# Row norm, turning and first products of eight stages put into one block each, tile by tile

## The reference: a network of four graph layers and four expert layers

```python
def _layernorm(x, axis=-1, eps=1e-05):
    m = jnp.mean(x, axis=axis, keepdims=True)
    v = jnp.var(x, axis=axis, keepdims=True)
    return (x - m) / jnp.sqrt(v + eps)
...
x = x + _L0_gnn_ref(_layernorm(x, axis=-1), edge_index, ...)
x = x + _L0_ffn_ref(_layernorm(x, axis=-1)[None], ...)[0]
x = x + _L1_gnn_ref(_layernorm(x, axis=-1), edge_index, ...)
x = x + _L1_ffn_ref(_layernorm(x, axis=-1)[None], ...)[0]
x = x + _L2_gnn_ref(_layernorm(x, axis=-1), edge_index, ...)
x = x + _L2_ffn_ref(_layernorm(x, axis=-1)[None], ...)[0]
x = x + _L3_gnn_ref(_layernorm(x, axis=-1), edge_index, edge_attr_256, ...)
x = x + _L3_ffn_ref(_layernorm(x, axis=-1)[None], ...)[0]
```

## Time and profile before

| | us |
|---|---|
| time before, median of 3 runs | 6647.78 |
| lowest and highest run | 6633.71, 6653.32 |
| span of the profiled execution | 6654.2 |
| PE busy in it | 4985.8 (75%) |
| DVE busy | 4006.3 (60%) |
| POOL busy | 2796.2 (42%) |
| ACT busy | 2392.6 (36%) |

### The profile page before, as it was taken

How to read it: one execution, slowest core, us unless ns; L and a number is a source line. 1 busy time by engine, 2 the same in 40 slices (tenths; PEclk the granted TensorE clock), 3 DMA queues, 4 the chain that set the end, 5 groups by cost and what they waited for, 6 DMA issues and landing times. The chain is left out here.

```text
span 6654.2 us, 84797 instructions
## 1 busy us (share of the span) xinstructions
PE 4985.8 (75%) x21057; PEld 3321.4 (50%) x21058; DVE 4006.3 (60%) x8393; ACT 2392.6 (36%) x5749; POOL 2796.2 (42%) x2895
## 2 busy tenths in 40 slices
PE   0677669458778667757775788889889994667998
PEld 0444336334436534433343444467678884455776
DVE  5577823457783467766777788821357775892112
ACT  0333312123332234423442555522135552552333
POOL 1577332447740077717771677700047673000000
PEclk9799869779998889988997899989999997897999
DMA  4444233234430144434441222100079995541000
GB/s 92 127 136 135 59 93 119 74 106 136 135 78 15 40 133 136 135 74 133 135 133 36 43 36 36 26 13 13 27 244 352 352 351 132 179 150 11 14 9 24
DMA packets 455531, 711.59 MB, mean 107 GB/s; under 512 B 105113, under 2 KB 334038, under 8 KB 455014
## 3 DMA queue, kind: packets, MB, share of 16 engines
q0 software_dynamic: 142432, 380.88, 21.1%
q1 hardware_dynamic: 310442, 318.36, 15.3%
q10 hardware_dynamic: 2304, 8.52, 0.3%
HBM read 604.94 MB, written 102.97 MB: 106 GB/s over the span
## 5 line engine op out<-in xcount | busy, mean ns | idle before, releaser
L666 POOL DMA_INDIRECT l_edges_stage<-l_h_rows,src_t x832 | 799.3, 961 | 329.7 <-issue 250.4
L2169 POOL DMA_INDIRECT l_edge_kv<-l_kv_rows,src_t x416 | 463.9, 1115 | 751.1 <-POOLq L2082 557.3
L904 PE MATMUL l_edges_ps_sum<-l_edges_msg,l_edges_hot 128*128 128x264 f32 x1664 | 541.2, 449 | 176.5 <-DVE l_attn_acc L776 87.3
L2605 POOL DMA_INDIRECT l_gate_edges_srow<-l_gate_src_rows,l_gate_edges_idx x512 | 483.6, 944 | 249.4 <-issue 155.7
L904 PEld LDWEIGHTS l_edges_ps_sum<-l_edges_msg,l_edges_hot 128*128 128x128 f32 x1664 | 281.1, 201 | 457.1 <-DVE l_attn_acc L776 319.8
L2741 PE MATMUL l_gate_edges_ps<-l_gate_edges_wide,l_gate_edges_hot_lo 128*128 128x500 f32 x1024 | 449.6, 593 | 79.0 <-DVE l_gate_edges_wide L2667 79.0
L666 POOL DMA_INDIRECT l2b_edges_stage<-l2b_h_rows,src_t x416 | 400.9, 964 | 168.7 <-issue 121.1
L666 POOL DMA_INDIRECT l2a_edges_stage<-l2a_h_rows,src_t x416 | 399.4, 960 | 165.1 <-issue 121.7
L776 DVE TENSOR_TENSOR l_attn_acc<-l_attn_acc,l_edges_ps_sum 128x264 f32 x832 | 350.4, 421 | 82.1 <-DVE l_attn_acc L776 37.9
L2270 PE MATMUL l_edge_ps_e<-l_edge_w,l_edge_eaT 128*128 128x256 f32 x1664 | 377.3, 380 | 0.0
L2390 DVE SCALAR_TENSOR_TENSOR l3f_acc<-l_experts_psb,l3f_g,l3f_acc 128x256 f32<-128x256 f32 x200 | 96.7, 484 | 444.6 <-PE l_experts_psb L2421 444.4
(11 more groups left out here) (772 smaller groups left out, 10771.9 us busy)
## 6 DMA issues: line engine op xcount, KB each, us to landing
l_val_rows<-l_edge_vj SPq DMA_DIRECT2D x104, 512.0 KB, 5.6
l_agg_stage<-l_val_rows SPq DMA_DIRECT2D x52, 1024.0 KB, 5.5
l_edge_ea<-in_edge_attr SPq DMA_DIRECT2D x388, 128.0 KB, 5.0
l_edges_rel_b<-rel_rows SPq DMA_DIRECT2D x52, 512.0 KB, 4.1
l_experts_w<-in_L_ffn_w SPq DMA_DIRECT2D x32, 512.0 KB, 4.7
l_gate_edges_lo_b<-l_gate_edges_lo_rows SPq DMA_DIRECT2D x64, 256.0 KB, 3.2
l_edges_stage<-l_h_rows,src_t POOLq DMA_INDIRECT x832, 2.8
l2a_edges_rel_b<-rel_rows SPq DMA_DIRECT2D x26, 512.0 KB, 4.0
```

Of the source, the lines that this page charges most:

```text
L666: nc.gpsimd.indirect_dma_start(out=stage[:, c % SL, u, :], out_offset=None, in_=h_rows, in_offset=bass.IndirectOffsetOnAxis(ap=K.src_t[:, ...
L904: nc.tensor.matmul(ps_sum[u][:], hot[:, g, u, :], msg[:, g % 2, u, :], start=True, stop=True).then_inc(summed, 1)
L2169: nc.gpsimd.indirect_dma_start(out=kv[:, m, u, :], out_offset=None, in_=kv_rows, in_offset=bass.IndirectOffsetOnAxis(ap=K.src_t[:, n * EB ...
L2605: nc.gpsimd.indirect_dma_start(out=srow[:, n % 4, u, :], out_offset=None, in_=src_rows, in_offset=bass.IndirectOffsetOnAxis(ap=idx[:, n * ...
```

## The change

`norm_and_transpose` and the block behind it become one block at the eight places. A class `TileNorm` holds the pieces of the norm as methods, and each engine's list calls them between its own work:

- The 25 tiles fall in two groups, of 10 and of 15 (`NORM_GROUPS`). `bn_stats`, `row_scales` (with its wait for ACT's root) and the normed tiles are done for the first group, then for the second, so each small instruction of `row_scales` runs twice, on [128, 10] and [128, 15].
- PE turns two tiles ahead (`AHEAD` is 2): before product t it turns tile t+2, which waits for the normed tile (`xn_ready`) and for a free one of 3 PSUM buffers; product t waits until tile t is copied (`kept`).
- The loads that SP starts come at the beginning of the joint block. DVE's preparation of weights stands between the two groups in `project` and `gate_nodes`.
- The copies that ACT makes stand in straight lines instead of hardware loops, and so do DVE's.

The core of the diff:

```diff
+HEAD_TILES = 10
+AHEAD = 2
+NORM_GROUPS = [range(0, HEAD_TILES), range(HEAD_TILES, NT)]
...
+class TileNorm:
...
+    def rows(self, dve, g):
+        ts = self.groups[g]
+        at = slice(ts[0], ts[-1] + 1)
+        dve.wait_ge(self.stats_done, ts[-1] + 1)
+        row_scales(self.nc, dve, self.chain, self.var_ready, self.std_ready, self.eps, self.stat[:, at, :],
+                   self.mean[:, at], self.rstd[:, at], self.a[:, at], self.b[:, at], g + 1)
+        for t in ts:
+            self.nc.vector.tensor_scalar(self.xn[:, t, :], self.y[:, t, :], self.mean[:, t:t + 1], self.rstd[:, t:t + 1],
+                                         ALU.subtract, ALU.mult).then_inc(self.xn_ready, 1)
+
+    def root(self, act, g):
+        at = slice(self.groups[g][0], self.groups[g][-1] + 1)
+        act.wait_ge(self.var_ready, g + 1)
+        self.nc.scalar.activation(self.b[:, at], self.a[:, at], ACT.Sqrt).then_inc(self.std_ready, 1)
+
+    def turn(self, pe, t, ready=True):
+        if ready:
+            pe.wait_ge(self.xn_ready, t + 1)
+        if t >= len(self.ps):
+            pe.wait_ge(self.kept, t + 1 - len(self.ps))
+        for c in range(DC):
+            last = self.nc.tensor.transpose(self.ps[t % len(self.ps)][:, c, :], self.xn[:, t, c * P:(c + 1) * P], self.ident)
+        last.then_inc(self.turned, 1)
+
+    def keep(self, act, t):
+        act.wait_ge(self.turned, t + 1)
+        self.nc.scalar.copy(self.xnT[:, :, t * P:(t + 1) * P], self.ps[t % len(self.ps)][:]).then_inc(self.kept, 1)
```

The lists of DVE, PE and ACT in `norm_project`, which was `project`:

```diff
+                if norm:
+                    nt.stats(dve, 0)
                 ch.note(nc.vector.memset(adp[:, NT], 0.0))
+                if norm:
+                    nt.rows(dve, 0)
                 dve.wait_ge(w_in, 16 * w_loads(w_view))
...
                     nc.vector.tensor_copy(to, frm).then_inc(w_ready, 1)
+                if norm:
+                    nt.stats(dve, 1)
+                    nt.rows(dve, 1)
                 dve.wait_ge(h_kept, NT)
...
+                for t in range(AHEAD):
+                    nt.turn(pe, t, norm)
                 pe.wait_ge(w_ready, 2)
                 for t in range(NT):
+                    if t + AHEAD < NT:
+                        nt.turn(pe, t + AHEAD, norm)
+                    pe.wait_ge(nt.kept, t + 1)
...
+                for t in range(NT):
+                    if t + AHEAD < NT:
+                        if norm and t + AHEAD == HEAD_TILES:
+                            nt.root(act, 1)
+                        nt.keep(act, t + AHEAD)
+                    act.wait_ge(projected, t + 1)
```

The lists of ACT and DVE in `node_projections`:

```diff
+                for t in range(NT):
+                    if t == 0:
+                        nt.root(act, 0)
+                    if t == AHEAD:
+                        nt.root(act, 1)
+                    nt.keep(act, t)
...
+                for g in range(len(NORM_GROUPS)):
+                    nt.stats(dve, g)
+                    nt.rows(dve, g)
+                dve.wait_ge(nt.xn_ready, NT)
                 dve.wait_ge(w_in, 32 * len(order))
```

## The result

| | before | after |
|---|---|---|
| time, median of 4 runs, us | 6646.66 (6633.71 to 6653.32) | 6588.01 (6585.56 to 6589.60) |
| span of the profiled execution, us | 6654.2 | 6587.2 |

The ratio is 0.9914, with a 95% interval of 0.9900 to 0.9928: 59 us less in the medians. The forecast was 6588.0.

What follows compares the result with a forecast made beforehand. Eight places, each a chain mostly without a second engine beside it, took about 465 of 6654 us. Gains of 63.9 us, less 3 for the clock, left 60: median 6647.8 to 6588, range 6552 to 6618.

Steps and rivals of the forecast that it cites:

- What bounds: Eight places are chains mostly without a second engine beside them, about 465 us of 6654, all the change can touch.
- The start of l0, l1, l2a: In these projections PE may start its first product 12.9 us in, after statistics, small instructions, ten normed tiles and weights' preparation.
- The price of a turn: Turning one tile between two products costs PE 0.17 us at the full clock, 0.32 at the low clock.
- The stand at tile 10: In l0, l1, l2a PE stands 2.8 us, since the second root waits on ACT behind the copies of product 7.
- The slow clock at the start: First products in the projections run slow, costing 2.1 us in l0, 3.1 in l1, 2.0 in l2a, 2.7 in l2b.
- The clock after the stand: PE's wait may let the clock fall again, up to 2.1 us in each of three projections; half, 3 us, taken.
- Routers and gate nodes: Routers of l0 and l3 end at 39.0 us against 47.0, at 1.18 a tile; gate nodes 41.7 against 47.3.
- Layer 3: Its projections' product 2 waits for DVE's additions until 24.7 us; the end comes at 109.4 against 118.1, 8.7 less.
- The sum: Gains over all places add to 63.9 us; less 3 for a falling clock, about 60 remain.
- The fast routers: Rival: the clock rises in routers and gate nodes, 34 us more gain, time 6554; chance 0.10.
- dearer beyond the bound: Rival: interleaving costs more, by the upper bounds in most places, 20 to 35 us less gain, 6608 to 6623; chance 0.17.
- the clock stay low in the projections: Rival: PE stays at 0.50 in the projections, 60 us gained and 186 lost, time near 6774; chance 0.02.

Runs made afterwards that it cites:

- the three cases named above: Joint block only in projections (0.9970), only in routers and gate nodes (0.9980), or everywhere with one group of 25 tiles (0.9963), each ratio against the kernel before.

## Why the prediction was right, point by point

- **What bounds.** From one variant to the next the time followed the sum of the eight places, within 5 us in the medians of three chips, and within 10 in the three cases named above.
- **The start of l0, l1, l2a.** First product at 12.7 us, forecast 12.9. Two errors met: the small instructions got 0.7 us shorter, where I had kept their price, and the turn of tile 2 stands between the wait for the weights and product 0, which I had left out.
- **The price of a turn** I took as 0.17, with bounds of 0 and 0.32, from the records that touch 1 us in the earlier trace rows. Counted by their starts, as shown above, the same records say 0.22 at clock 1.00 and 0.43 at 0.50. At the full clock a turn between products does cost 0.22, and the error of 0.05 x 23 = 1.1 us in each of four projections and in layer 3 makes 6 us in all. At clock 0.50 a turn costs 0.43 in the projections (2.24 from product 0 to 1, where two slow products of the kernel before start 1.81 apart), but in the routers only 1.17 - 0.85 = 0.32. There the misread 0.32 was right by luck. With 0.22 and 0.43 in its sums the forecast would have been some 13 us higher, near 6601 (an estimate: 6 us and 0.11 x 23 in each of three places).
- **The stand at tile 10.** Forecast 2.8, measured 2.23 in the projections, and its cause proved right when the root was moved. In the routers it was 19.6 - 17.4 = 2.2 by the forecast and is 1.49.
- **The slow clock at the start** was taken over from the kernel before: 2.1, 3.1, 2.0 and 2.7 us in l0, l1, l2a and l2b. It cost 1.8, 2.6, 1.2 and 1.6, by the distances of the first products over 1.14, so 2.7 us less in all. In five other traces that enter the projections the same way it was 1.2 to 2.6 in l0, so the size that it had here is luck, and it hid more than half of the 4.6 us by which the turns in the projections were dearer. In l2b it made up for turns that were 1.1 us dearer and a start at 8.1 instead of 7.5.
- **The clock after the stand.** I had taken half of 2.1 us in three places, 3. In l0 and l2a it fell, at (1.74 - 1.14) + (2.21 - 1.14) = 1.7 us in l0 and as much in l2a, in l1 not: 3.3 in all.
- **Routers and gate nodes.** Tile 1.17 (forecast 1.18) at clock 0.50. They gained 25.0 us where 21.6 were forecast: the first product came at 7.7 instead of 8.2 and the stand was shorter.
- **Layer 3.** Product 2 started at 23.2 instead of 24.7, since the small instructions of both groups got shorter. What was mis-sized is the slow clock. I charged 1.7 us, the slow start of the kernel before. The slow start itself cost nothing here, since products 0 and 1 had time until product 2 could go, but behind the stand the clock was low again and cost 6.72 - 3.67 = 3.05. With 1.0 for the dearer turns, 1.4 for the clock and 1.5 the other way, 110.3 came out instead of 109.4.
- **The sum** was 60.9 and the places gave 62.7. The errors were of both signs and up to 1.9 us a place. The mechanism was right in every place; that its terms cancelled so well is luck.
- **The rivals.** The fast routers did not come, nor did any tile get dearer beyond the bound, nor did the clock stay low in the projections, which ran 1.14 us a tile for most of their length.
- **The rule on transposes.** "TensorE: Matmul & The Clock Gate", Part 4, of the Trainium skill would keep the full clock away from transpose mode. The earlier trace rows spoke against it, and no run here has brought a case for it: the routers stay at 0.50, but the earlier trace rows shows the same clock for their narrow products without any turn between them, so turning is not needed to explain it.

## What to carry to other kernels

When a wait moves into a joint block, look for what the engine that must answer it has ahead of it in its own list. Here one small instruction of ACT, placed three or four tiles too late, cost 2.2 us of PE in each of three stages and a slow clock behind it in ten of fifteen. Moving it shortened the places by another 13 to 15 us beside the 63 of the change. In layer 3, starting the bounding engine earlier was worth nothing, since it then had to stand for another engine's list. Where an engine waits anyway and its clock has fallen, dense work right ahead of the real work gave the slow start back in the cases in which it ended at most 1.9 us before it, and not in the two in which it ended 2.8 and 3.3 us before. And when a window view counts records that touch a stretch, take prices from their starts, not from that count.

## What the runs showed of the hardware that was not expected

- The clock's fall after a stand of 2.23 us went with what was before it. In the fifteen normed projections with the stand in five traces it fell in ten and not in five. In all four in which products 0 and 1 both were fully slow (2.24 us each) it did not fall; in the other eleven, where the clock had risen earlier, it fell ten times. The same code in one execution has both cases: l0 fell, l1 did not. Why is not shown.
- Two turning records start 0.11 us apart at clock 1.00, between products as well as when nothing else runs. At clock 0.50 they start 0.21 apart alone, so a tile takes 0.43 us, but among the narrow products of a router a turned tile adds only 0.32.
- Narrow float32 products with turns and with a bf16 product of 512 columns in each tile leave the clock at 0.50 for 40 us, in which PE stands once for 1.07 us and three times for 0.2.
- One chip made the program 22% longer, in the stages with gathers above all, while each of the places, which have none, kept its length to about 1.5 us.
